# Remainders of the last three weight units computed by GpSimd instead of VectorE

## The reference, cut to what matters

```python
x = x + _L0_xattn_ref(_layernorm(x, axis=-1), ctx_4096, ...)
x = x + _L0_attn_ref(_layernorm(x, axis=-1), Wq, Wk, Wv, Wo)
x = x + _L0_ffn_ref(_layernorm(x, axis=-1), ...)

# _L0_attn_ref, 32 heads of 32, 8 key heads
q = (x @ Wq.T); k = (x @ Wk.T); v = (x @ Wv.T)
q = q * cos + _rotate_half(q) * sin
scores = where(causal, q k^T / sqrt(32), min); attn = softmax(scores)
out = attn v
return out @ Wo.T
```

## Time and profile before

| | us |
|---|---|
| median of 3 runs | 1132.21 |
| lowest and highest | 1131.28, 1133.27 |
| the profiled execution, its own time | 1133.6 |
| its span | 1131.7 |
| TensorE busy | 1064.2 |
| VectorE busy | 828.8 |
| ScalarE busy | 476.6 |
| GpSimd busy | 159.1 |

### The profile page before, as it was taken

The page is one execution under the profiler, slowest core; times in us unless marked ns, Lnnn a source line. Parts: engine busy times, 40 slices in busy tenths (PEclk is TensorE's granted clock), DMA queues, the critical chain, the costliest instruction groups (busy, mean ns, idle before and its releaser), DMA issues.

```text
span 1131.7 us, 17533 instructions
## 1 busy us (share of the span) xinstructions
PE 1064.2 (94%) x6308; PEld 894.0 (79%) x6308; DVE 828.8 (73%) x1886; ACT 476.6 (42%) x1012; POOL 159.1 (14%) x162
## 2 busy tenths in 40 slices
PE   4999999999999999999999999999999999898736
PEld 3888888788888887888888887888888788787525
DVE  6787668676767868766678876675547798837998
ACT  4553434444444456454544454441224334321315
POOL 0000000322332232332333220000001000000000
PEclk9999999999999999999999999999999999989778
DMA  9785775244443333344445313899835313000001
GB/s 234 154 202 126 160 162 137 67 109 98 107 107 74 75 70 75 77 106 107 93 95 109 69 25 72 174 217 242 176 75 107 62 30 48 2 14 1 1 1 74
DMA packets 184540, 111.26 MB, mean 98 GB/s; under 512 B 108040, under 2 KB 174344, under 8 KB 184480
## 3 DMA queue, kind: packets, MB, share of 16 engines
q1 hardware_dynamic: 182224, 109.37, 44.9%
q10 hardware_dynamic: 2256, 1.11, 0.5%
HBM read 90.98 MB, written 18.94 MB: 97 GB/s over the span
## 4 chain that ended last, share of the span: by engine, by line
PE 83%; DVE 13%; ACT 2%; issue 1%; DMA 1%; ACTq 0%; POOL 0%; DVEq 0%
PE ps L606 29%; PE ps L513 15%; PE ps L573 13%; PE ps L939 9%; PE ps L499 4%; PE ps L617 4%; PE ps L634 4%; DVE wt L1501 1%; DVE small L2051 1%; DVE small L2055 1%; DVE small L2043 1%; DVE small L2047 1%; PE ps L717 1%; DVE small L2039 1%; DVE small L2035 1%
## 5 line engine op out<-in xcount | busy, mean ns | idle before, releaser
L606 PE MATMUL ps<-wt,act 128*128 128x512 f32 x1536 | 381.0, 394 | 0.0
L606 PEld LDWEIGHTS ps<-wt,act 128*128 128x128 f32 x1536 | 278.1, 188 | 51.8 <-issue 0.4
L513 PE MATMUL ps<-wt,act 128*128 128x512 f32 x768 | 177.3, 392 | 3.7 <-DVE wt L1501 3.7
L513 PEld LDWEIGHTS ps<-wt,act 128*128 128x128 f32 x768 | 144.7, 189 | 34.2 <-DVE act L1485 4.1
L573 PE MATMUL ps<-act,wt 128*128 128x512 f32 x672 | 153.7, 390 | 0.0
L573 PEld LDWEIGHTS ps<-act,wt 128*128 128x128 f32 x672 | 125.8, 188 | 26.0
L1056 ACT ACTIVATE wt<-raw 128x512 fp32r<-128x512 f32 x192 | 106.3, 625 | 92.4 <-PE ps L513 52.4
L1501 DVE TENSOR_TENSOR wt<-raw,wt 128x512 fp32r<-128x512 f32 x192 | 120.0, 682 | 25.9 <-ACT wt L1056 25.9
L939 PE MATMUL ps<-wt,act 128*128 128x512 f32 x480 | 124.5, 409 | 0.6 <-DVE wt L1501 0.6
L1493 DVE STREAM_TRANSPOSE raw<-raw 128x1024 f32<-128x1024 f32 x92 | 107.9, 1217 | 21.9 <-DMA raw<-in_L_xattn_o_proj_w 21.9
L2202 POOL TENSOR_TENSOR small<-small 128x4 f32<-128x4 f32 (+2 forms) x64 | 68.8, 1077 | 286.2 <-DVE small L1515 214.0
(11 more groups left out here) (161 smaller groups left out, 1205.2 us busy)
## 6 DMA issues: line engine op xcount, KB each, us to landing
xr<-in_ctx SPq DMA_DIRECT2D x64, 256.0 KB, 4.9
raw<-in_L_xattn_o_proj_w SPq DMA_DIRECT2D x32, 512.0 KB, 14.3
raw<-in_L_xattn_q_proj_w SPq DMA_DIRECT2D x28, 512.0 KB, 9.4
xr<-q_rows SPq DMA_DIRECT2D x16, 512.0 KB, 4.2
ot_hi<-spare SPq DMA_DIRECT2D x64, 128.0 KB, 2.0
act<-ot_hi SPq DMA_DIRECT2D x32, 256.0 KB, 9.3
q_rows<-G SPq DMA_DIRECT2D x28, 256.0 KB, 2.8
raw<-in_L_xattn_k_proj_w SPq DMA_DIRECT2D x8, 512.0 KB, 6.8
```

Source lines behind the costliest of these rows:

```text
L513: mm = pe.matmul(banks[t], lhs(p == 2, c, t), wt[:, n_slot, int(p == 1), c, :], start=(acc_from and q == 0), stop=(acc_to and q == 3 * NC ...
L606: mm = pe.matmul(bank, src[int(p == 2)][:, c, kt * P:(kt + 1) * P], wt[:, slot, int(p == 1), c, :], start=(q == 0), stop=(q == 3 * NC - 1))
```

## The change

The 24 subtractions that make the remainders of units 22, 23 and 24 leave VectorE's order, and GpSimd gets them: first the units 22 and 23, then the setting of `ones` that was there, then unit 24, then the roots. Each still waits for its chunk's high part, and signals `w_lo`. Before the first, GpSimd waits for the end of unit 21's remainders, which stay with VectorE.

```diff
@@ -1925,8 +1925,6 @@
             turns = {1: (23, (0, 1)), 4: (23, (2,)), 5: (23, (3,)), 8: (24, (0, 1)), 9: (24, (2, 3))}
-            later = {1: (22, (0, 1, 2)), 2: (22, (3, 4, 5)), 3: (22, (6, 7)), 4: (23, (0, 1)), 5: (23, (2, 3)),
-                     6: (23, (4, 5)), 7: (23, (6, 7)), 9: (24, (0, 1, 2, 3)), 10: (24, (4, 5, 6, 7))}
             def add_last(t, half):
@@ -1950,9 +1948,6 @@
                 if b in turns:
                     for j in turns[b][1]:
                         turn_unit(turns[b][0], j)
-                if b in later:
-                    for c in later[b][1]:
-                        lo_unit(later[b][0], c)
                 if 3 <= b <= 10:
                     lo_out2(b - 3)
@@ -2255,8 +2250,20 @@
             for k in range(NT, 2 * NT):
                 ln_root(k)
                 ln_move(k)
+
+            def lo_unit(n, c):
+                pool.wait_ge(w_hi, NC * n + c + 1)
+                pool.tensor_tensor(blocks16(wt[:, n % 2, 1, c, :]), raw_chunks(raw_slot(n), c),
+                                   blocks16(wt[:, n % 2, 0, c, :]).bitcast(F32), ALU.subtract).then_inc(w_lo, 1)
+
+            pool.wait_ge(w_lo, NC * 22)
+            for n in (22, 23):
+                for c in range(NC):
+                    lo_unit(n, c)
             pool.wait_ge(qt_done, 8)
             pool.memset(ones, 1.0).then_inc(ones_ready, 1)
+            for c in range(NC):
+                lo_unit(24, c)
             for t in range(NT):
                 pool.wait_ge(z_var, t + 1)
```

## The result

The changed kernel takes 1129.18 us (median of 7 runs, 1127.29 to 1132.39), the kernel before in as many runs 1133.27 (1131.28 to 1135.3). The ratio on record is 0.9969, with a 95% interval of 0.9954 to 0.9984: 3.5 us, or 0.3%, faster. The profiled execution is one run of the seven. The two profiled spans differ by 3.9 us, 1131.7 and 1127.8.

The account below looks back on a forecast made before the run. VectorE was nearly full, but relief paid only where TensorE waited, in tiles 1, 2 and 9. Terms +1.19 + 1.59 - 0.42 - 1.90 - 2.77 = -2.3 us, gain taken as 2.2 from 1132.2: 1130.0 us, range 1126.7 to 1133.0.

Parts of the forecast that it names:

- What bounds it, and where it pays: Self-attention tiles: VectorE nearly full, but relief pays only where TensorE waits: 1.81 us tile 1, 0.84 tile 2, 2.49 tile 9.
- Tile 9: `lo_out2` starts 2.37 us earlier without four subtractions ahead, less 0.47 for L1868 held by GpSimd: -1.90 us.
- The clock in tiles 9 and 10: Tiles 9 and 10: no clock fall behind the smaller gaps, so 0.80 and 1.97 us are won back: -2.77.
- the second rival: Tile 9: clock stays low or a new gap replaces the old; +0.5 us or nothing, 1132.5 us; chance 0.10.
- Tile 2: Rotation and exponential for tile 2 come 0.42 us earlier; slower tile 1 matmuls make L1850 miss the burst: -0.42 us.
- the other branch: Tile 2 without tile 1's clock fall: L1850 ready at 911.2 and held 0.8 us, net +0.4.
- Tile 1's hold: Tile 1: L1850 comes 0.09 us after GpSimd's third operation starts and is held to its end: +1.19 us.
- The clock in tile 1: Tile 1: clock falls behind TensorE's gap of 3.0 us, slowing 12 matmuls from 3.01 to 4.60: +1.59 us.
- The first rival, VectorE is not held: Tile 1: VectorE gets the ports or only GpSimd waits; -5.6 to -4.3 us, 1126.6 to 1127.9 us; chance 0.33.
- The third rival, a dearer chunk: GpSimd chunk near 2.40 us instead of 1.28, delaying tiles 1, 9, 10; about +4 us, 1136 us; chance 0.07.
- The sum: Whole kernel: hold, clock, tile 2 and tile 9 terms give -2.3 us, from 1133.6 to 1131.3 us profiled.

Follow-up runs that it names:

- Unit 24 alone: Against the kernel before, only unit 24's remainders go to GpSimd, those of units 22 and 23 stay on VectorE: 1127.55 us, ratio 0.9961.
- units 22 and 23: Against the kernel before, remainders of units 22 and 23 go to GpSimd, unit 24's stay on VectorE: 1132.18 us, ratio 0.9994.
- the order alone: Against the kernel before, `lo_out2` goes ahead of the four remainders in tile 9, all remainders stay on VectorE: 1128.96 us, ratio 0.9968.
- the repeat: The changed kernel as it stands, run again beside other experiments on one chip: 1129.25 us, ratio 0.9967 to the kernel before.

## Why the prediction was right, and where not

- *What bounds it, and where it pays*: right. Unit 24 alone gives the whole gain, units 22 and 23 none, and the order alone gives it with no work taken off. The prediction named the cause (four remainders ahead of `lo_out2`), but not that the order alone would do. TensorE waited for none of GpSimd's remainders in the profile.
- *Tile 9*: -1.90 predicted, -2.29 measured: 0.20 of the gap was left. L1868 was to be held 0.47 and was held 0.11. In part that is chance: TensorE's stall for instructions at the start of the tile was 1.12 us here and 0.88 before, so L1868 came 0.24 later against the burst. In the repeat the stall was 0.82, the hold 0.43 and the gap 0.52, near the forecast.
- *The clock in tiles 9 and 10*: -2.77 predicted, -2.79 measured. The clock stayed up there in both profiles of the change, so the second rival (it stays low) is refuted.
- *Tile 2*: -0.42 predicted, -0.44 measured, by the path that was named: the slower matmuls of tile 1 take L1850 out of the burst's way. The repeat, without them, shows the other branch: held by 0.67, and a gap of 1.06, +0.22 where the prediction had +0.4.
- *Tile 1's hold*: +1.19 predicted, +0.28 measured. The step that failed is GpSimd's start. I had it 0.08 us behind ScalarE's high part, from rows in the first stage; here it came near 0.5 behind it (902.07, where the first of three high parts that begin at 900.94 and take 0.62 each ends at 901.56), after an idle time of 32.7 us. So the third operation had not begun when L1850 came; L1850 waited 0.26 for the second, and the third waited for L1850: the longest of GpSimd's operations is 1.73 us, where the others take 1.28.
- *The clock in tile 1*: a fall was predicted behind a gap of 3.0 us. It came behind one of 2.09 and cost 1.60, as priced. In the repeat there was none, so this term is a chance and no constant, and that it came is in part luck.
- *The first rival, VectorE is not held*: refuted. L1850, 0.69 us alone, took 0.95, 1.53, 1.36, 1.19 and 1.84 us beside GpSimd, and 0.69 in the kernels where GpSimd was idle there. Rows 8 showed one direction; these show the other. How long the hold is can be read off as well. This is the GpSimd operation that L1850 (904.19, 0.95 us) met in tile 1:

```profile
903.31 1.28 POOL L2256 TENSOR_TENSOR wt<-raw,wt 128x512 fp32r<-128x512 f32 x1
```

  It ends at 904.59 and L1850 0.55 us later. All nine held L1850 of these traces end 0.55 us behind the GpSimd operation, all twelve held L1868 and L1842 (1024 elements) 1.08 us behind it: 0.14 less than each takes alone. So VectorE is held for what is left of the operation, less 0.14 us; the prediction took the whole of what is left. In the other direction, a GpSimd operation that began while L1850 ran took 1.70 to 1.84 us instead of 1.28.

  The Trainium skill ("SBUF — State Buffer", Who interferes with whom) says that a VectorE instruction with two SBUF inputs contends with a GpSimd instruction that reads SBUF, over a pair of ports that is an exclusive lock. The traces agree in both directions.
- *The third rival, a dearer chunk*: refuted. A chunk takes 1.28 to 1.29 us (the middle value of each group), as estimated:

```profile
L2256 POOL TENSOR_TENSOR wt<-raw,wt x16: 1258/1291/1734, 902.1 to 993.4; 128x512 fp32r<-128x512 f32 x16
L2256 POOL TENSOR_TENSOR wt<-spare,wt x8: 1261/1280/1290, 929.7 to 960.9; 128x512 fp32r<-128x512 f32 x8
```

- *The sum*: -2.3 us against a profiled difference of -3.9 and a measured one of -3.5. Against the profile 0.9 lies in tile 1's hold and 0.4 in tile 9; the 1.58 of tile 5 and the 1.9 of the last tile were in no term and nearly cancel. The first comes with the execution: the clock fell in tile 5 in the profile before and in none of the later ones. That the forecast of 1130.0 us lies so near the measured 1129.18 is in part luck: it started from a median of 1132.2 us over three runs, where seven give 1133.27, and the gain itself was forecast at 2.2 us and measured at 3.5.

What stays open: why GpSimd's first operation starts late, what decides whether the clock falls behind a gap of 2 us, and what puts the fall near the last tile ahead of its last groups or behind them.

## What to carry to other kernels

When an engine is nearly full, look first at what TensorE waits for and what stands just ahead of that on the full engine; reordering four instructions gave here what moving 24 gave. Work given to GpSimd in bursts holds a VectorE instruction with two SBUF inputs that comes during it, by 0.1 to 1.15 us here and never by more than what was left of one GpSimd operation, so put the bursts where VectorE has none, or where its result isn't waited for. A gap of some 2 us of TensorE can cost 1.6 us more through the clock, but not in every execution: take such a term from several profiles.

## What was not expected of the hardware

- GpSimd's first operation after 32.7 us of idling or more began 0.5 us behind the end of the instruction that released it in five profiles (at 902.07 in the changed kernel); after 5 us of idling the delay was about 0.1.
- The lower clock came behind gaps of 2.09 and 2.08 us and stayed away behind another of 2.08, with the same work around. It also came behind stalls for instructions of 1.28 and 1.43 us among small matmuls, and not behind others of 1.28, 1.40 and 1.56. Each of these four falls cost 1.6 us.
- A VectorE instruction held by GpSimd ends a fixed time behind the GpSimd operation: 0.55 us for 128x512 and 1.08 for 128x1024, in all 21 holds of these traces.
